# Feed-forward stage: the last tile of 32 rows folded on three partition groups, with own buffers, and the end of the stage written out call by call

## The reference

```
def fp4_linear(x, w):
    xq = fp4_quant_dequant(x)      # blocks of 16 values along the last dim:
    wq = fp4_quant_dequant(w)      # scale = max|block| / 6, round to 8 levels, times scale
    return jnp.einsum('bsk,nk->bsn', xq, wq)
gate = fp4_linear(x, w_gate)       # 256 -> 704
y = fp4_linear(x, w_up)            # 256 -> 704
h = jax.nn.silu(gate) * y
return fp4_linear(h, w_down)       # 704 -> 256
...
h = h + ffn(_layernorm(h), w_gate, w_up, w_down)
```

## Time and profile before

| | us |
|---|---|
| median of 3 runs | 536.42 (536.14 to 537.23) |
| profiled execution, time | 535.42 |
| profiled execution, span of its instructions | 533.7 |

### The profile page before, as it was taken

One profiled execution on the slowest core, in us unless ns is written; L12 is line 12 of the kernel. 1 busy time (PEld: TensorE's weight loads), 2 busy tenths in 40 slices (PEclk: granted clock), 3 DMA queues, 4 the chain that ended last, 5 costly groups with the idle time before them and its releaser, 6 DMA issues.

```text
span 533.7 us, 13792 instructions
## 1 busy us (share of the span) xinstructions
PE 493.7 (93%) x3628; PEld 400.4 (75%) x3628; DVE 472.8 (89%) x1267; ACT 329.5 (62%) x752; POOL 272.0 (51%) x365
## 2 busy tenths in 40 slices
PE   6959899879999999999999979899999999999966
PEld 4748666557777777777776667788888888888965
DVE  2688999979999999999999799999999999999961
ACT  6654776757777777877777859454545445454420
POOL 2486656545444544455446255555555555555540
PEclk9988999999999999999999989999999999999987
DMA  8910010111111111111121210212212211221111
GB/s 275 335 39 28 13 37 29 35 57 49 49 52 52 52 47 49 52 46 50 46 65 44 50 36 27 76 43 59 59 49 59 59 50 48 59 59 49 41 39 43
DMA packets 31914, 32.13 MB, mean 60 GB/s; under 512 B 4144, under 2 KB 30096, under 8 KB 31888
## 3 DMA queue, kind: packets, MB, share of 16 engines
q1 hardware_dynamic: 31888, 31.82, 20.0%
HBM read 23.09 MB, written 8.71 MB: 60 GB/s over the span
## 4 chain that ended last, share of the span: by engine, by line
PE 69%; DVE 11%; issue 4%; ACT 2%; DMA 0%; POOL 0%; DVEq 0%; SPq 0%; ACTq 0%; POOLq 0%
PE bank L153 28%; PE bank_a L153 16%; PE bank L795 5%; PE bank L807 4%; PE bank L1447 4%; PE bank L786 4%; PE bank L820 2%; PE bank_b L838 2%; PE bank_a L754 1%; PE bank_b L1455 1%; PE bank_a L758 1%; DVE bank L1233 1%; DVE var L983 1%; DVE fh L1221 0%; ACT pt L883 0%
## 5 line engine op out<-in xcount | busy, mean ns | idle before, releaser
L883 ACT ACTIVATE pt<-bank 113x452 f32<-113x452 f32 x128 | 60.9, 553 | 38.5 <-PE bank L795 38.2
L1301 POOL TENSOR_TENSOR h_deq<-fh,fhb 128x704 f32<-128x704 f32 x29 | 40.4, 1392 | 67.2 <-DVE fhb L1172 64.7
L153 PE MATMUL bank<-wgu_hi,fx_hi 128*128 128x512 f32 x174 | 66.8, 384 | 1.8 <-DVE fx_lo L1225 1.8
L153 PE MATMUL bank<-wgu_lo,fx_hi 128*128 128x512 f32 x174 | 66.1, 380 | 0.0
L153 PE MATMUL bank<-wgu_hi,fx_lo 128*128 128x512 f32 x174 | 66.0, 379 | 0.0
L960 POOL TENSOR_TENSOR rope<-rope 113x512 f32<-113x512 f32 x32 | 41.3, 1292 | 32.7 <-DVE rope L999 32.5
L953 POOL TENSOR_TENSOR rope<-rope,columns 113x256 f32<-113x256 f32 x64 | 48.8, 779 | 16.2 <-DVE rope L991 16.2
L153 PE MATMUL bank_a<-wd_hi,fh_hi 128*128 128x256 f32 x174 | 53.6, 308 | 2.3 <-DVE res L1179 2.3
L153 PE MATMUL bank_a<-wd_hi,fh_lo 128*128 128x256 f32 x174 | 50.6, 291 | 0.0
L153 PE MATMUL bank_a<-wd_lo,fh_hi 128*128 128x256 f32 x174 | 50.5, 290 | 0.0
L153 PE MATMUL bank<-wqkv_hi,xo_hi 128*113 128x512 f32 (+1 forms) x128 | 47.5, 371 | 3.1 <-DVE wgu_lo L465 2.5
(11 more groups left out here) (181 smaller groups left out, 1501.8 us busy)
## 6 DMA issues: line engine op xcount, KB each, us to landing
xb<-h_dram SPq DMA_DIRECT2D x29, 129.0 KB, 2.1
rb<-h_dram SPq DMA_DIRECT2D x29, 128.0 KB, 2.1
h_dram<-h SPq DMA_DIRECT2D x32, 112.9 KB
out<-res SPq DMA_DIRECT2D x28, 128.0 KB, 1.7
px<-in_patches SPq DMA_DIRECT2D x9, 384.0 KB, 9.4
hx<-in_txt SPq DMA_DIRECT2D x32, 77.0 KB
hr<-in_txt SPq DMA_DIRECT2D x32, 77.0 KB
wf<-in_wgu SPq DMA_DIRECT2D x1, 1408.0 KB, 14.0
```

The costliest lines, as they stand in the source:

```text
L153: last = pe.matmul(dst, a(k), w(k), start=(start and n == 0), stop=(n == len(passes) - 1))
L883: act.activation(pt[0:T, r, :, :].rearrange("p s t -> p (s t)"), sc_ps[r][0:T, :], ACT.Exp, scale=1.0 / math.sqrt(HD)).then_inc(m["exp_mad ...
L1301: pool.tensor_tensor(blocks(h_deq[:, 0:INTER], BLK), blocks(h_code[:], BLK), spread(h_scale[:], BLK), ALU.mult).then_inc(f["h_deq"], 1)
```

## The change

Tile 28 gets its own form (`small(s)`), for which `COLS` is 256 and `GROUPS` is 3.

- The 704 hidden values of its 32 rows are folded: values 0 to 255 on partitions 0 to 31, 256 to 511 on 32 to 63, and 512 to 703 on 64 to 95. All elementwise steps of the hidden part run on 96 partitions and 256 columns (`of`, `of_blocks`).
- To have TensorE put them there, the stationary operand of gate and up is 96 columns wide and holds the 32 columns of x at the place of the group and zeros elsewhere. It is cut as a window of `diag_hi` and `diag_lo`, which GpSimd zeroes once (`zero_diagonals`) and into which `x_high` and `x_low` write x three times. All groups add up in one PSUM tile for gate and one for up: `small_columns(s, n)` has 3 groups x 2 chunks x 3 passes = 18 matmuls each for gate (n = 0) and up (n = 1), of 256, 256 and 192 columns.
- Two transposes of 96 x 128 take the place of six; the down product takes 32-column pieces of the transposed tile as the stationary operand, 18 matmuls of 256 columns.
- The tile has its own `small_hi`, `small_lo`, `small_rb`, `small_res` and own places in PSUM, and leaves out the waits that protect the shared ones.

The loop now runs `t` from 5 to 23, and the rest is written out call by call for each engine in `tensor_end`, `vector_end`, `scalar_end`, `gpsimd_end` and `sync_end`, in an order that differs from that of the lists.

```diff
+COLS = 2 * P
+GROUPS = (INTER + COLS - 1) // COLS
...
+        small_hi, small_lo = sb("small_hi", [P, 2, GROUPS * LAST], F32R), sb("small_lo", [P, 2, GROUPS * LAST], F32R)
+        small_rb, small_res = sb("small_rb", [LAST, D]), sb("small_res", [LAST, D])
+        diag_hi, diag_lo = (sb(f"diag_{n}", [P, KD, GROUPS * P], F32R) for n in ("hi", "lo"))
...
+        small_loaded, diag_zeroed = sem("f_small_loaded"), sem("f_diag_zeroed")
+        small_xt = fxt_ps.rearrange("p (k n) -> p k n", k=KD)[:, :, 0:LAST].unsqueeze(2).broadcast_to([P, KD, GROUPS, LAST])
+        small_gate_up = [bank4[:, n, 0:COLS] for n in range(2)]
+        small_ht, small_down = bank4[:, 2, 0:2 * GROUPS * LAST], bank4[0:LAST, 0, 0:D]
...
+            return tile[:].rearrange("p k (g n) -> p k g n", g=GROUPS)[:, :, :, 0:LAST]
+
+        def of(tile, s):
+
+            return tile[0:GROUPS * LAST, 0:COLS] if small(s) else tile[:, 0:INTER]
+
+        def of_blocks(tile, s):
+
+            return tile[0:GROUPS * LAST, 0:COLS // BLK] if small(s) else tile[:, 0:NB_H]
...
+                if small(s):
+                    sp.dma_start(small_rb[:], h2_dram[s * P:s * P + LAST, 0:D]).then_inc(small_loaded, 16)
+                    return
                 after(sp, f["out_made"], s)
                 sp.dma_start(rb[:], h2_dram[bass.ds(s * P, P), 0:D]).then_inc(f["r_loaded"], 16)
 
...
-                sp.dma_start(out[bass.ds(s * P, rows), :], res[0:rows, :]).then_inc(f["stored"], 16)
+                if small(s):
+                    sp.dma_start(out[s * P:s * P + LAST, :], small_res[:]).then_inc(f["stored"], 16)
+                else:
+                    sp.dma_start(out[bass.ds(s * P, P), :], res[:]).then_inc(f["stored"], 16)
...
 
                 dve.wait_ge(f["down_made"], s + 1)
+                if small(s):
+                    dve.wait_ge(small_loaded, 16)
...
+                    pool.memset(tile[:].bitcast(F32), 0.0).then_inc(diag_zeroed, 1)
+
             def h_dequantise(s):
 
...
+                if small(s):
+                    act.activation(small_hi[:].rearrange("p k n -> p (k n)"), small_ht, ACT.Copy).then_inc(f["ht_high"], 1)
+                    return
...
+                act.activation(of(gate, s), of(small_gate_up[0], s) if small(s) else gate_ps, ACT.Silu).then_inc(f["silu_made"], 1)
...
+                if small(s):
+                    act.wait_ge(diag_zeroed, 2)
+                    act.activation(diagonal(diag_hi), small_xt, ACT.Copy).then_inc(f["xt_high"], 1)
+                    return
...
+            def small_columns(s, n):
+
+                if n == 0:
+                    pe.wait_ge(f["xt_low"], s + 1)
+                    pe.wait_ge(f["silu_made"], s)
+                else:
+                    pe.wait_ge(f["hidden_made"], s)
+                rows = GROUPS * LAST
+                passes = [(x, w, k, g) for g in range(GROUPS) for k in range(KD)
+                          for x, w in ((diag_hi, wgu_hi), (diag_hi, wgu_lo), (diag_lo, wgu_hi))]
+                for i, (x, w, k, g) in enumerate(passes):
+                    at, width = n * INTER + g * COLS, min(COLS, INTER - g * COLS)
+                    mm = pe.matmul(small_gate_up[n][0:rows, 0:width], x[:, k, g * rows:(g + 1) * rows],
+                                   w[:, k, at:at + width], start=(i == 0), stop=(i == len(passes) - 1))
+                mm.then_inc(f["up_made" if n else "gate_made"], 1)
+
             def h_transposes(s):
 
+                if small(s):
+                    pe.wait_ge(f["h_deq"], s + 1)
+                    rows = GROUPS * LAST
+                    for j in range(2):
+                        mm = pe.transpose(small_ht[:, j * rows:(j + 1) * rows], h_deq[0:rows, j * P:(j + 1) * P],
+                                          ident[0:rows, 0:rows])
+                    mm.then_inc(f["ht_made"], 1)
+                    return
...
+                if small(s):
+                    pe.wait_ge(f["ht_low"], s + 1)
+                    passes = [(a, w, k) for k in range(KI)
+                              for a, w in ((small_hi, wd_hi), (small_hi, wd_lo), (small_lo, wd_hi))]
+                    for i, (a, w, k) in enumerate(passes):
+                        rows, c = min(P, INTER - k * P), slice(k // 2 * LAST, (k // 2 + 1) * LAST)
+                        mm = pe.matmul(small_down, a[0:rows, k % 2, c], w[0:rows, k, :], start=(i == 0),
+                                       stop=(i == len(passes) - 1))
+                    mm.then_inc(f["down_made"], 1)
+                    return
...
+        def tensor_end(pe, f):
+
+            f.first_columns(24); f.middle_columns(24); f.last_columns(24); f.x_transposes(25); f.h_transposes(22)
+            f.down(21); f.first_columns(25); f.middle_columns(25); f.last_columns(25); f.h_transposes(23)
+            f.x_transposes(26); f.down(22); f.first_columns(26); f.middle_columns(26); f.last_columns(26)
+            f.h_transposes(24); f.x_transposes(27); f.down(23); f.first_columns(27); f.middle_columns(27)
+            f.last_columns(27); f.h_transposes(25); f.x_transposes(28); f.down(24); f.small_columns(28, 0)
+            f.h_transposes(26); f.down(25); f.small_columns(28, 1); f.down(26); f.h_transposes(27)
+            f.h_transposes(28); f.down(27); f.down(28)
...
+        def vector_end(dve, f):
+
+            f.h_low(21); f.x_maxima(26); f.rows_out(20); f.x_inverse(26); f.hidden(24); f.x_low(25); f.h_rounded(23)
+            f.x_rounded(26); f.h_codes(23); f.h_scales(23); f.x_codes(26); f.h_maxima(24); f.x_scales(26)
+            f.h_inverse(24); f.x_maxima(27); f.h_low(22); f.x_inverse(27); f.rows_out(21); f.hidden(25)
+            f.h_rounded(24); f.x_low(26); f.h_codes(24); f.h_scales(24); f.h_maxima(25); f.x_rounded(27)
+            f.h_inverse(25); f.x_codes(27); f.h_low(23); f.x_scales(27); f.rows_out(22); f.x_maxima(28)
+            f.hidden(26); f.h_rounded(25); f.x_low(27); f.h_codes(25); f.x_inverse(28); f.h_scales(25)
+            f.h_maxima(26); f.rows_out(23); f.h_inverse(26); f.x_rounded(28); f.h_low(24); f.x_codes(28)
+            f.x_scales(28); f.hidden(27); f.h_rounded(26); f.h_codes(26); f.h_scales(26); f.x_low(28)
+            f.h_maxima(27); f.h_inverse(27); f.h_low(25); f.rows_out(24); f.h_rounded(27); f.rows_out(25)
+            f.h_codes(27); f.h_scales(27); f.h_low(26); f.hidden(28); f.h_maxima(28); f.h_inverse(28)
+            f.rows_out(26); f.h_rounded(28); f.h_codes(28); f.h_scales(28); f.h_low(27); f.h_low(28); f.rows_out(27)
+            f.rows_out(28)
...
+        def scalar_end(act, f):
+
+            f.x_norm(26); f.h_high(21); f.silu(24); f.x_high(25); f.h_magnitude(23); f.x_magnitude(26); f.x_norm(27)
+            f.h_high(22); f.silu(25); f.h_magnitude(24); f.x_high(26); f.x_magnitude(27); f.h_high(23); f.x_norm(28)
+            f.silu(26); f.h_magnitude(25); f.x_high(27); f.h_high(24); f.x_magnitude(28); f.silu(27)
+            f.h_magnitude(26); f.x_high(28); f.h_high(25); f.h_magnitude(27); f.silu(28); f.h_high(26)
+            f.h_magnitude(28); f.h_high(27); f.h_high(28)
+
+        def gpsimd_end(pool, f):
+
+            f.zero_diagonals(); f.h_dequantise(22); f.x_dequantise(25); f.h_quotient(23); f.x_quotient(26)
+            f.h_dequantise(23); f.x_dequantise(26); f.h_quotient(24); f.x_quotient(27); f.h_dequantise(24)
+            f.h_quotient(25); f.x_dequantise(27); f.x_quotient(28); f.h_dequantise(25); f.h_quotient(26)
+            f.x_dequantise(28); f.h_dequantise(26); f.h_quotient(27); f.h_dequantise(27); f.h_quotient(28)
+            f.h_dequantise(28)
+
+        def sync_end(sp, f):
+
+            f.load_residual(21); f.store(20); f.load(27); f.load_residual(22); f.store(21); f.load(28); f.store(22)
+            f.load_residual(23); f.load_residual(24); f.store(23); f.load_residual(25); f.store(24); f.store(25)
+            f.load_residual(26); f.store(26); f.load_residual(27); f.load_residual(28); f.store(27); f.store(28)
...
-            with engine.Fori(5, FT - 3) as t:
+            with engine.Fori(5, 24) as t:
                 tiles(t)
-            for t in range(FT - 3, FT + 4):
-                tiles(t)
+            end(engine, tile_stages)
```

More of the change, by code:

```diff
@@ L1116, in early_fusion, with small, diagonal @@
         f = {n: sem("f_" + n) for n in names.split()}
+        small_loaded, diag_zeroed = sem("f_small_loaded"), sem("f_diag_zeroed")
+        small_xt = fxt_ps.rearrange("p (k n) -> p k n", k=KD)[:, :, 0:LAST].unsqueeze(2).broadcast_to([P, KD, GROUPS, LAST])
+        small_gate_up = [bank4[:, n, 0:COLS] for n in range(2)]
+        small_ht, small_down = bank4[:, 2, 0:2 * GROUPS * LAST], bank4[0:LAST, 0, 0:D]
+        def small(s):
+            return isinstance(s, int) and s == FT - 1
+        def diagonal(tile):
+            return tile[:].rearrange("p k (g n) -> p k g n", g=GROUPS)[:, :, :, 0:LAST]
[3 more added lines that the diff above has]
+            return tile[0:GROUPS * LAST, 0:COLS // BLK] if small(s) else tile[:, 0:NB_H]
```

(22 more changed lines are left out.)

43 lines of the change are left out of this document (24 added, 19 removed).

## The result

| | before | after |
|---|---|---|
| median us | 536.83 (4 runs, 536.14 to 537.29) | 528.25 (4 runs, 527.38 to 528.97) |
| ratio after / before | | 0.9844 (95%: 0.9827 to 0.9862) |
| profiled execution, time and span | 535.42, 533.7 | 528.96, 527.0 |
| instructions | 13792 | 13748 |

By the ratio, the change makes the kernel 8.4 us faster (1.6%; its interval is 7.4 to 9.3 us). The forecast was 527.6.

The account below looks back on a forecast made before the run. VectorE was taken to pace the loop, TensorE the written-out tiles, and waits plus slow clock the drain. Layout against layout, 533.1 - 524.3 = 8.8 us, subtracted from the 536.4 median, gave 527.6 us; range 526.0 to 531.0.

Parts of the forecast that it names:

- the two layouts: Old and new call orders laid out on five engines with durations from rows: ends at 533.1 and 524.3, 8.8 us apart.
- Loop: Tiles 24 and 25 taken out of the loop: two periods of 7.20 become 6.85, 0.7 us less.
- The wait before tile 23's transposes: In the new order h_transposes(23) waits 0.55 us for h_low(22), which now stands after the inverses.
- The fold: Tile 28 on 256 columns and 96 rows; full-size steps put back would end the new order's layout 5.6 us later.
- the 0.36 kept as a bound: Tile 28's twelve 192-column products held at 0.12 us by operand loads would cost 0.36 us; 0 was taken.
- the slower rival: Tile 28's 54 narrow products each wait for load and drain, 0.4 to 0.5 us each, ending at 546; chance 0.04.
- The neighbour that the prediction leaned on: The 32-wide stationary operand of L807: 16 products of 226 columns in 0.97 us, 0.06 each, read as against slow loads.
- Own buffers: Before the last down: no wait for rows_out(27) and an early residual, said to remove the 2.28 us wait.
- the sum against the trace: Drain, loop and transposes: 12.8 us of savings less 3.7 of new waits, 9.1 us; not the figure taken.
- second round: On VectorE, rows_out(26) ahead of h_rounded(28) delays the end likewise; 1 us on it and on rows_out(25) gives 529.6.
- rival 2: A new-order wait replaces those removed, as rows_out(25) ahead of h_codes(27): 529.6, or 530.4 with half the fold's gain lost; chance 0.16.
- The clock: Drain: 4.6 us of slow products removed, clock holding; rival: a fall behind the 1.6 us gap, 529.2 to 531.1, chance 0.23.

Follow-up runs that it names:

- unroll24: The kernel before with its loop ended two tiles earlier and nothing else changed: ratio 0.9988 to the kernel before.
- written_out: The changed kernel with the remaining 19 loop turns (tile steps 5 to 23) also written out: 521.26 us, ratio 0.9705 to the kernel before.
- codes_low_first: The changed kernel with h_codes(27), h_scales(27) ahead of rows_out(25), h_high(22) ahead of x_norm(27), h_low(22) ahead of x_maxima(27): ratio 0.9818 to the kernel before.
- full_in_new_order: The changed kernel with tile 28 back on full-size steps and shared buffers, new order kept: ratio 1.0037 to the kernel before.
- shared_buffers: The changed kernel with tile 28's last down product, residual and result back in the shared buffers with their waits: ratio 0.9837 to the kernel before.
- filler: The kernel before with 53 useless matmuls put into TensorE's three waits in the drain: ratio 0.9926 to the kernel before.
- control: The changed kernel itself, unaltered and measured again: 527.62 us against 536.04, ratio 0.9852 to the kernel before.

## Why the prediction came out right, point by point

**The sum of the drain.** Forecast 8.8 us less by the two layouts; the stretch is 8.8 shorter (54.69 to 45.87). Counted from 476.68, the layout had 521.96 - 476.68 = 45.3 for it, 0.6 too short, and it was 0.6 too short for the old order as well (533.1 for 533.7), so the difference of layouts was the right thing to take. That it fits to 0.1 us is partly luck, since single terms below are off by 0.2 to 0.5 and the stretch itself is only good to 0.25.

**Loop.** 7.20 to 6.85 a tile: unroll24 measures 0.75 for two tiles and written_out 7 to 8 us for 19 more. The reading of the two periods holds. Which part of it is the waits against registers and which the branch was not tested. That the 7.20 leave 6.8 us on the table in the rest of the loop was in the rows and not drawn out of them.

**The wait before tile 23's transposes.** 0.55 was forecast and 0.72 came, with the columns of tile 26 7.73 behind those of tile 25 instead of 7.4. The size was off because of a step that the layout had only in passing: `load(27)` stands on SP behind `load_residual(21)` and `store(20)`, its data came 3.64 us after the issue, and ScalarE had `x_norm(27)` ahead of `h_high(22)` (ScalarE waited 2.8 us for it). codes_low_first takes that away.

**The fold.** The text put it at 5.6 us, as tile 28's chain alone at full size. Undone as a whole in this order it costs 9.7 (55.57 - 45.87), so the term was much too small. About 3.0 of the 9.7 are the clock: in full_in_new_order the last transposes take 1.54 and the last two downs 2.77 and 3.78, where 0.66, 2.11 and 2.28 stand at full rate. The shared buffers are undone with it, and their wait of 2.28 stands there again. How the rest divides was not separated. Added alone to the old order the fold brings 4.3. The two don't add up as separate terms. The new order without the fold loses 0.9, the fold without the order brings 4.3, both together 8.8; the loop's 0.75 is in the first and the third of these. Part of what the two bring together is the clock: the products behind the last gap run at 2.4 GHz in five of six profiled executions that have it.

**Operand loads.** 0.12 us for 256 columns and 0.08 to 0.09 for 192, so neither the 0.36 kept as a bound nor the slower rival (0.4 to 0.5 for each) appeared. The neighbour that the prediction leaned on does not bear this out, though: 226 columns take 226 / 256 x 0.117 = 0.10 us one after another, and the earlier trace rows shows 0.06, so those products overlap. In the program, four in a row write four different groups of 32 partitions of one tile. That the narrow products here step at 0.12 is shown by their own rows alone. Whether the 96-wide operand changes a tiling mode is not shown; whatever the steps into the new products cost, the trace puts an upper end on it. The first 96-wide product steps 0.20, as the first of each full down does (504.94 to 505.14), and the step from the downs of tile 27 into the 32-wide ones shows no wait. The step into the 64-row products costs 0.1 us, which no term of the sum had.

**Zeroing.** 0.74 us each (0.83 forecast), hidden, as said.

**Own buffers.** Here a term of the sum was wrong. The 2.28 us wait before the last down was counted as theirs. shared_buffers shows a wait of 0.52, and 0.7 us in the end: with the products close to each other only one add lies between. Most of the wait went because the drain got short; the buffers hold a quarter of it. Only the sum against the trace (9.1) has this term by itself, and it was not the one taken.

**What VectorE waits for.** The text had `rows_out(25)` wait for the landing of `store(24)`. The timeline says 0.73 us for PE bank_a, the product of tile 25 itself. The store was issued at 510.30, and by the 1.7 us of the earlier trace rows it had landed at 512.0, before the product ended at 512.67. The place in VectorE's queue, with `h_codes(27)` behind it, was right; moving the codes ahead brings the drain about 0.3 us forward. The cause was wrong: the layout had the product of tile 25 end at 510.1 (505.0 + 1.93 + 0.36 + 0.66 + 2.11) and the landing at 510.4, and in the trace the product was the later of the two. The "second round" of the prediction's rival 2 also came, at a small size. ScalarE ended `h_magnitude(28)` at 516.91 + 0.42 = 517.33, but `h_rounded(28)` started at 517.77, behind `rows_out(26)`, which waited 1.25 us for the product of tile 26 (lines above). The chain of waits goes this way: down(26), `rows_out(26)`, `h_rounded(28)`, `h_dequantise(28)`, and so into the gap of 1.48.

**The clock.** Forecast to hold with one gap of 1.6 us, with 0.23 for a fall and 1.6 us as its price. It held in the two executions of the change and fell once in six with that gap. There it cost 1.3 us on down(27) and 0.2 on down(28). The 4.6 us counted for the old drain are 4.0 to 4.2 by filler.

**The end.** The last add starts at 524.64, where 521.96 was laid out. 0.6 of this is the stretch. The other 2.1 us come from before it, where no line of the program differs: the columns of tile 24 start at 478.77 (476.68 before). The two kernels are within 0.02 us of each other up to 307 us and part in the transition from attention to feed-forward. The windows of TensorE there, before (it stays at 1.00 from 317 to 347) and then after (1.00 from 307 to 317):

```profile
307.00:312.00 5.00, 2.69 (x8) 0.78 0.23 64
312.00:317.00 5.00, 4.22 (x22) 0.88 0.08 24
317.00:322.00 5.00, 4.84 (x26) 1.00 0.17 50
```

```profile
317.00:322.00 5.00, 5.00 (x18) 0.66 0.20 50
...
337.00:342.00 5.00, 3.88 (x20) 0.66 0.37 106
```

Before, the clock is under 1.00 for the parts that the values 0.78 and 0.88 give, (0.22 + 0.12) x 5 / 0.5 = 3.4 us at 1.2 GHz, at a place with few products. After, it is twice 0.34 x 5 / 0.5 = 3.4 us, with TensorE at work in both, and TensorE ends this part 2.1 us later. This is no effect of the change: in the control, the same kernel, the columns of tile 24 start at 477.14, and in the eleven profiled executions whose program is the same up to there they start anywhere from 476.15 to 478.84. The four executions of the change have spans of 525.5, 525.5, 526.9 and 527.0; that the transition parts these is likely and not shown. The median came out 0.65 above the forecast for a plainer reason: 0.4 is the kernel before, whose median moved from 536.42 to 536.83 with a fourth run, and 0.2 is that the two medians differ by 8.6. Medians of one kernel vary by 1 us, so a closer fit than this would have been luck.

## What to carry to other kernels

A ragged last tile that is computed with all its columns costs the elementwise engines as much as a full one, and its chain lies bare at the end. Folding it on idle partitions pays if TensorE can place it for nothing, as it could here. Order and fold have to be made together, since each alone brought half or a loss. Compare the period in a loop with the one in its written-out copy before tuning anything else: 0.37 us a turn was worth nearly as much here as the whole change.

## What the runs showed that I had not expected

- Matmuls of no use, put into the waits of a drain, made the kernel 4.0 us faster (0.9926), since the clock stayed at 2.4 GHz.
- The same gap of 1.48 us was followed by 2.4 GHz in five profiled executions and by 1.2 GHz in one; a gap of 2.46 also passed without a fall.
- Writing out a loop of 19 turns cost 14 more packets of instructions and no stall that the trace shows.
- In the transition the place of the slow clock differs between executions of the same instructions: by 2.1 us at its end between before and after, by 1.6 us between two executions of the change.
